# Scan stage of a hybrid block: the normalised inputs join the output product on TensorE instead of being summed into X by GpSimd, and four inputs are turned at other units

## What is computed

```python
def _L0_attn_b_ref(x, W_in, conv_w, conv_b, W_x, W_dt, b_dt, A_log, D, W_out):
    residual = x
    h = x
    for i in range(N_LAYERS):
        h = _mamba_layer(h, W_in[i], ...)
    return h + residual
...
x = x + _L0_attn_b_ref(_layernorm(x, axis=-1), ...)
```

```python
xz = jnp.einsum('bld,ed->ble', x, W_in)
u, z = jnp.split(xz, 2, axis=-1)
u = _silu(_causal_conv1d(u, conv_w, conv_b))
x_dbl = jnp.einsum('bld,rd->blr', u, W_x)
dt, Bm, Cm = jnp.split(x_dbl, [DT_RANK, DT_RANK + D_STATE], axis=-1)
dt = jax.nn.softplus(jnp.einsum('blr,dr->bld', dt, W_dt) + b_dt)
# per state n of 16: h = exp(dt*A)*h + dt*B*u ;  y = sum over n of h*C
y = _selective_scan(u, dt, A, Bm, Cm, Dvec)
y = y * _silu(z)
return jnp.einsum('bld,od->blo', y, W_out)
```

## Time and profile before

| | us |
|---|---|
| median of 3 runs | 2099.44 (2098.75 to 2099.64) |
| the profiled execution, its own time | 2099.91 |
| span of the profiled execution | 2098.1 |
| attention and first mixture of experts | 0 to about 764 |
| scan stage | about 764 to 1551 |
| second mixture of experts | 1551 to the end |

### The profile page before, as it was taken

How to read it: one execution, slowest core, us unless ns; L and a number is a source line. 1 busy time by engine, 2 the same in 40 slices (tenths; PEclk the granted TensorE clock), 3 DMA queues, 4 the chain that set the end, 5 groups by cost and what they waited for, 6 DMA issues and landing times. The chain is left out here.

```text
span 2098.1 us, 43518 instructions
## 1 busy us (share of the span) xinstructions
PE 2017.1 (96%) x14806; PEld 1576.1 (75%) x14807; DVE 1455.4 (69%) x2683; ACT 1202.9 (57%) x2403; POOL 1439.2 (69%) x973
## 2 busy tenths in 40 slices
PE   7999999999999989999999999999799999999998
PEld 5887447999999736666676666666564499999994
DVE  6887685333333389999999999999976733333335
ACT  5775522222222259999999999999853232222222
POOL 6775004777777439999999999999940077777760
PEclk9999999999999999999999999999999999999999
DMA  8000100000000344433444334333343000000014
GB/s 312 1 0 2 41 1 15 25 25 25 25 25 24 83 123 119 112 103 113 113 112 114 122 112 112 107 112 108 102 178 116 3 25 25 25 25 25 24 24 124
DMA packets 94714, 151.21 MB, mean 72 GB/s; under 512 B 27611, under 2 KB 61789, under 8 KB 92422
## 3 DMA queue, kind: packets, MB, share of 16 engines
q1 hardware_dynamic: 85510, 131.10, 20.7%
q0 software_dynamic: 9088, 18.63, 3.1%
...
## 5 line engine op out<-in xcount | busy, mean ns | idle before, releaser
L2413 POOL TENSOR_TENSOR m_seen<-m_state,experts 128x1024 f32<-128x1024 f32 (+1 forms) x256 | 598.8, 2375 | 12.3 <-DVE m_state L2468 10.3
L2468 DVE TENSOR_TENSOR_SCAN m_state<-experts,ps 128x512 f32<-128x512 f32 x448 | 537.2, 1233 | 1.9 <-issue 1.3
L1940 PE MATMUL ps<-ident,m_seen 128*128 128x128 f32 x2040 | 270.5, 276 | 23.7 <-POOL m_seen L2413 23.6
L2204 ACT ACTIVATE experts<-delta,experts 128x512 f32<-128x512 f32 x448 | 291.4, 713 | 0.3
L1940 PEld LDWEIGHTS ps<-ident,m_seen 128*128 128x128 f32 x2040 | 234.6, 142 | 63.1 <-POOL m_seen L2413 45.0
L1600 POOL COPY f_weights<-experts 128x1898 f32 x142 | 252.5, 1778 | 23.8 <-issue 23.5
L1421 PE MATMUL first_up_ps<-f_xT,f_weights 128*128 128x128 f32 x1988 | 241.4, 275 | 1.7 <-issue 1.7
L1421 PE MATMUL ps<-zu,f_weights 128*128 128x128 f32 x1988 | 241.4, 275 | 1.7 <-issue 1.7
L1421 PEld LDWEIGHTS first_up_ps<-f_xT,f_weights 128*128 128x128 f32 x1988 | 233.2, 192 | 2.5 <-issue 2.5
L1421 PEld LDWEIGHTS ps<-zu,f_weights 128*128 128x128 f32 x1988 | 233.2, 192 | 2.5 <-issue 2.5
L1588 POOL DMA_INDIRECT f_xin<-tokens,f_take x71 | 70.8, 997 | 153.0 <-DVE f_take L1124 134.6
...
## 6 DMA issues: line engine op xcount, KB each, us to landing
...
```

Source lines behind the costliest of these rows:

```text
L1940: mm = pe.matmul(Y[:, i // 2, at:at + P], seen[:, n % SEEN, h, i * P:(i + 1) * P], ident[:], is_transpose=True, start=(n == 0 and at == 0) ...
L2204: act.activation(PB[n % B_RING][:, h, :] if n in AWAY else dA[:, n % DECAYS, h, :], delta[:, U % 2, h, :], ACT.Exp, scale=decay[:, lhn:lhn ...
L2413: pool.tensor_tensor(seen[:, n % SEEN, :, part], state[:, n % RING, :, part], row.unsqueeze(1).to_broadcast([P, HALF, row.shape[-1]]), ALU ...
L2468: dve.tensor_tensor_scan(state[:, n % RING, h, :], decay_, drive_, before_, ALU.mult, ALU.add).then_inc(s_state, 1)
```

## The change

- `add_input` is gone, on POOL, with its two calls at the head and its six at step 13 of units 0 to 5, and so are the semaphore `s_added` and all waits on it.
- In `project_out` of an upper unit PE adds the normalised input from xT, where it still lies turned: for each of the four tiles a matmul with the turned input as weights and the identity as the moving operand, ahead of the one that adds X. `last_out` gets one such matmul for each of its four tiles.
- Since xT holds one sequence per stream only, the inputs k = 4 to 7 must not overwrite it before the output product of the upper unit that needs the old contents. The table `TURNED_IN` gives the unit in which input k is normalised, turned and copied: k = 2 to 7 in units 0, 1, 4, 6, 8, 10 in place of 0, 1, 2, 3, 4, 5. `columns` waits for that output product.

```diff
@@ -1688,7 +1688,7 @@
                 s_w, s_skipped, s_zero, s_halves, s_first_dt = ts("w"), ts("skipped"), ts("zeroed"), ts("halves"), ts("first_dt")
                 s_stats, s_var, s_std, s_rstd = ts("stats"), ts("var"), ts("std"), ts("rstd")
                 s_exp_A, s_neg_A = ts("exp_A"), ts("neg_A")
-                s_ln, s_added = ts("ln"), ts("added")
+                s_ln = ts("ln")
                 s_side0, s_side1, s_read0, s_read1 = ts("side0"), ts("side1"), ts("read0"), ts("read1")
                 s_silu, s_rows, s_bc, s_rounded, s_less, s_parts = (ts(x) for x in ("silu", "rows", "bc", "rounded", "less", "parts"))
                 s_soft, s_dt, s_dtu = ts("soft"), ts("dt"), ts("dtu")
@@ -1711,6 +1711,7 @@
                 N_UNITS = len(UNITS)
                 STEPS = N_UNITS * NS
                 TURNS = len(lower)
+                TURNED_IN = {k - 2 if k < LEAD + 1 else 2 * (k - 2): k for k in range(2, TURNS)}
 
                 def tokens(s, t):
 
@@ -1756,8 +1757,8 @@
                     if V < N_UNITS:
                         uses0 += [("dt0", V), ("dt1", V), ("gate", V), ("b", V), ("du", V)]
                         uses1.append(("gate", V))
-                    if U + 2 < TURNS:
-                        uses1.append(("turn", U + 2))
+                    if U in TURNED_IN:
+                        uses1.append(("turn", TURNED_IN[U]))
                     if V < N_UNITS:
                         uses1.append(("du", V))
                 uses0.append(("out", N_UNITS - 1))
@@ -1962,6 +1963,11 @@
                                     mm = pe.transpose(SIDES[:, h, i * P:(i + 1) * P], turned[:, at:at + P], ident[:])
                             mm.then_inc(s_back, 1)
 
+                        def input_columns(s, t, i):
+
+                            at = PAD + t % C * SEG + i * P
+                            return xT[:, s, at:at + P]
+
                         def project_out(W):
                             l, s, t = UNITS[W]
                             pe.wait_ge(s_y, W + 1)
@@ -1973,7 +1979,8 @@
                                     for h in range(HALF):
                                         mm = pe.matmul(SIDE0[:, i * P:(i + 1) * P], y[:, h, i * P:(i + 1) * P], out_w[:, l * HALF + h, :], start=(h == 0), stop=(h == HALF - 1))
                                 if W < N_UNITS - 1:
-                                    pe.wait_ge(s_added, min(2 * t + s + 1, TURNS))
+                                    for i in range(TILES):
+                                        pe.matmul(SIDE0[:, i * P:(i + 1) * P], input_columns(s, t, i), ident[:], start=False, stop=False, skip_group_check=True)
                                     mm = pe.matmul(SIDE0, ident[:], X[:, tokens(s, t) * D:tokens(s, t) * D + SEG], start=False, stop=True, skip_group_check=True)
                             mm.then_inc(s_side0, 1)
 
@@ -2042,8 +2049,8 @@
                                     gate(V, 1)
                                 if n == B_TURN:
                                     turn_b(V)
-                            if n == TURN and U + 2 < TURNS:
-                                turn(U + 2)
+                            if n == TURN and U in TURNED_IN:
+                                turn(TURNED_IN[U])
                             if n == DU_TURN and V < N_UNITS:
                                 turn_delta_u(V)
                             if n == SKIP:
@@ -2094,7 +2101,8 @@
                             pe.wait_ge(s_y, LAST_UNIT + 1 + j)
                             for i in range(2):
                                 for h in range(HALF):
-                                    mm = pe.matmul(Y[:, j, i * P:(i + 1) * P], y[:, h, (2 * j + i) * P:(2 * j + i + 1) * P], out_w[:, l * HALF + h, :], start=(h == 0), stop=(h == HALF - 1))
+                                    pe.matmul(Y[:, j, i * P:(i + 1) * P], y[:, h, (2 * j + i) * P:(2 * j + i + 1) * P], out_w[:, l * HALF + h, :], start=(h == 0), stop=False)
+                                mm = pe.matmul(Y[:, j, i * P:(i + 1) * P], input_columns(*UNITS[LAST_UNIT][1:], 2 * j + i), ident[:], start=False, stop=True)
                             mm.then_inc(s_side0, 1)
 
                         def ahead_down(c):
@@ -2123,6 +2131,8 @@
                             at = PAD + t % C * SEG
                             bank, s_side, s_read, nth = (SIDE0, s_side0, s_read0, nth0) if k < 2 else (SIDE1, s_side1, s_read1, nth1)
                             act.wait_ge(s_side, nth["turn", k] + 1)
+                            if t >= C:
+                                act.wait_ge(s_side0, nth0["out", UNITS.index((1, s, t - C))] + 1)
                             act.activation(xT[:, s, at:at + SEG], bank, ACT.Copy).then_inc(s_read, 1)
 
                         def convolved(V, h):
@@ -2245,7 +2255,6 @@
 
                         def normalise(k):
                             l, s, t = lower[k]
-                            act.wait_ge(s_added, k)
                             act.wait_ge(s_shift, 1)
                             for i in range(TILES):
                                 j = tokens(s, t) + i
@@ -2259,7 +2268,6 @@
 
                         def normalise_group():
                             act.wait_ge(s_group_shift, 1)
-                            act.wait_ge(s_added, TURNS)
                             act.wait_ge(s_side1, nth1["turn", TURNS - 1] + 1)
                             for i in range(TILES):
                                 ins = act.activation(xn[:, i * P:(i + 1) * P], X[:, i * D:(i + 1) * D], ACT.Identity, scale=numbers[:, RSTD, i:i + 1], bias=numbers[:, SHIFT, i:i + 1])
@@ -2348,10 +2356,10 @@
                             if V < N_UNITS:
                                 if n in GATED:
                                     gated(V, GATED.index(n))
-                            if n == TURN - 1 and U + 2 < TURNS:
-                                normalise(U + 2)
-                            if n == TURN and U + 2 < TURNS:
-                                columns(U + 2)
+                            if n == TURN - 1 and U in TURNED_IN:
+                                normalise(TURNED_IN[U])
+                            if n == TURN and U in TURNED_IN:
+                                columns(TURNED_IN[U])
                             if n in ACROSS_AT:
                                 m = ACROSS_AT[n] + (NS if ACROSS_AT[n] < n else 0)
                                 if U * NS + m < STEPS:
@@ -2384,12 +2392,6 @@
                         pool.memset(diagonal[0], 0.0)
                         pool.memset(hT[:, :, 0:PAD], 0.0).then_inc(s_hT, 1)
 
-                        def add_input(k):
-                            l, s, t = lower[k]
-                            at = tokens(s, t) * D
-                            wait(pool, s_ln, k)
-                            pool.tensor_tensor(X[:, at:at + SEG], X[:, at:at + SEG], xn[:], ALU.add).then_inc(s_added, 1)
-
                         def drive(G):
                             U, n = divmod(G, NS)
                             pool.wait_ge(s_dtu, U + 1)
@@ -2397,8 +2399,6 @@
                             wait(pool, s_state, (G - DECAYS + 1) * HALF)
                             pool.tensor_tensor(dA[:, n % DECAYS], delta_u[:, U % 2], b_rep[:, AWAY.index(n), :].unsqueeze(1).to_broadcast([P, HALF, SEG]), ALU.mult).then_inc(s_away, 1)
 
-                        add_input(0)
-                        add_input(1)
                         pool.tensor_tensor(conv_w[:, 1], conv_w[:, 1], in_wT[:, DI:2 * DI].unsqueeze(1).to_broadcast([P, TAPS, DI]), ALU.mult).then_inc(s_hT, 1)
                         drive(AWAY[0])
                         for G in range(STEPS):
@@ -2422,8 +2422,6 @@
                             if n == DELTA_U and V < N_UNITS:
                                 pool.wait_ge(s_dt, V + 1)
                                 pool.tensor_tensor(delta_u[:, V % 2], delta[:, V % 2], u(V), ALU.mult).then_inc(s_dtu, 1)
-                            if n == TURN and U + 2 < TURNS:
-                                add_input(U + 2)
                             if U == N_UNITS - 1 and n == GROUP_STATS:
                                 group_statistics(pool, numbers, s_group, s_group_shift, summed[0] + TILES)
 
@@ -2435,7 +2433,6 @@
 
                         def normalise(k):
                             l, s, t = lower[k]
-                            dve.wait_ge(s_added, k)
                             for i in range(TILES):
                                 ins = layernorm(dve, xn[:, i * P:(i + 1) * P], tokens(s, t) + i)
                             ins.then_inc(s_ln, 1)
@@ -2533,7 +2530,6 @@
                         dve.wait_ge(made.s_down, 1)
                         ahead_product(dve, made, 2)
                         _, s, t = UNITS[LAST_UNIT]
-                        dve.wait_ge(s_added, TURNS)
                         for j in range(2):
                             at = tokens(s, t) + 2 * j
```

## The result

The changed kernel took 2100.77 us in the median of 22 runs (2098.09 to 2105.47), the kernel before 2097.63 us in the 22 runs beside it (2094.57 to 2101.40). The ratio is 1.0016, with a 95% interval from 1.0010 to 1.0022: about 3.4 us slower, and less than the 0.2% that I had set as the bound of "no change". The profiled execution took 2100.88 us, with a span of 2098.8. The forecast of 2100.2 stood against a kernel before of 2099.44; what it says of the change is +0.74 us, and that is 2.5 us too little.

What follows compares the result with a forecast made beforehand. No engine has room in the scan loop, so waits between engines set each unit's period. Terms -4.96 +2.06 +1.58 +1.09 +0.97 = +0.74 on 2099.91, less 0.47 for the median: 2100.2 us; range 2095.4 to 2104.0.

Steps and rivals of the forecast that it cites:

- GpSimd's sums: Scan loop: six sums at step 13 of units 0 to 5 go, 1.24 us each where GpSimd is the bound.
- 0→1: Period from unit 0's step-9 sum into delta to unit 1's: sum worth the 0.86 us gate wait, 47.91 to 47.05.
- 4→5: Period from unit 4's step 9 to unit 5's: sum goes, turn stays, at first -1.24 us.
- 2→3, 3→4, 5→6: Periods between step 9 of those units, which lose sum and turn: -1.24, -1.32 and -1.41 us.
- Moved turns: Turns leave units 2, 3, 5 for 6, 8, 10: +1.30 us in unit 6, -0.19 in unit 8, 0 in 10.
- Added matmuls: Upper units' output products at step 5: eight more passes, 0.97 us, delaying GpSimd's step-9 sum; +2.06 us in six units.
- Both together: Late ScalarE makes the turn later in units 6, 8 (+0.44 us) and 4, 10 (+1.14): +1.58 us.
- Head and tail: Stage's start: DVE's first statistic behind GpSimd's longer product, +1.09 us; last output product, 16 to 24 passes: +0.97.
- the second: Rival: added matmul passes come through whole, 0.97 us in each of six units, +4.50, 2103.9 us; chance 0.15.
- the third: Rival: one more fall of TensorE's clock in a bound unit of the loop, 2101.7 us; chance 0.10.
- The first: Rival: PE's added passes are covered before step 9, head perhaps free too, -3.99, 2095.4 us; chance 0.17.
- The fourth: Rival: moved turns cost nothing because GpSimd is behind anyway at steps 14 and 15, 2092.8 us; chance 0.05.

Runs made afterwards that it cites:

- e1: The kernel before without add_input's sums into X and their waits, turns unmoved, no added matmuls, normalised input left out of the result: 2097.11 us, ratio 0.9994.
- e2: The changed kernel without the added matmuls, normalised input left out of the result: 2097.73 us, ratio 1.0000.
- e3: The changed kernel with GpSimd's product on conv_w at the head waiting until VectorE's variances are done: 2099.92 us, ratio 1.0013.

## Why the prediction was right or wrong

- **The time** of 2100.2 lies 0.6 from the 2100.77 measured, partly by luck: the kernel before came out 1.8 us lower in the longer series than in the three runs I started from, and the change cost 3.1 to 3.4, not 0.74. Its class, within 0.2%, was right.
- **GpSimd's sums**, the step that failed. "The sum is worth what DVE waited at the gate, 0.86" for 0→1: it gained nothing. The wait in front of the gate product was ScalarE's work for the turned input, one link behind TensorE; "it waits so only when GpSimd is behind" was wrong. In 4→5 the sum was costed at 1.24, the distance between 2→3 and 10→11. But unit 2 has a sum and a turn and unit 10 neither, so this is the price of both: 0.82 for the sum (e1) and 0.43 for the turn (e2), which I had put at nothing. The missed amounts are 0.87 in 0→1, 0.62 in 4→5 and 0.60 in 10→11, 2.1 us, nearly all that the loop came out above the forecast apart from the clock.
- **2→3, 3→4, 5→6**: right in size, by comparing units of like kind, and not in the reason. What I took for turn and sum together in 3→4 and 5→6 was the turn alone, and what I took for the sum alone in 2→3 was 0.81 of sum and the rest turn (e1).
- **Moved turns**: 6→7 +1.44 for 1.52 forecast (turn and delay), and 1→2 unchanged; right. A new wait at the gate from unit 6 on, named as a sign of being wrong, is there but small: behind the moved turns TensorE stands 0.49 (units 7 and 9) and 0.63 (unit 11) for ScalarE at step 4, and VectorE 0.16 more at most.
- **Added matmuls**: 5→6 and 7→8 are 0.15 above the forecast, 3→4 and 9→10 within 0.03. In fresh even units the delay of TensorE comes through by 0.89, in continuing ones by 0.1, as the rooms in the earlier trace rows said. The first row that shows it, VectorE's stand at step 8, was not on my list, and step 9's room was not the place.
- **Both together**: too small. The matmuls cost 0.75 in 4→5 and 10→11 (e2), on top of 0.43 for the turn itself; I had 0.57 for the two. The 0.1 in the periods ahead, 3→4 and 9→10, is thus only what shows first.
- **The clock**: I counted the fall in 8→9 as gained (1.49 of the 48.57, so that the turn there came out at -0.19). It is no property of that unit. The changed kernel had two, in units 11 and 13.
- **Head and tail**: +0.91 and +0.88 for 1.09 and 0.97. For the head the cleaner figure is the first scan's +0.88, since the falls of the clock behind it move the head by up to 1.1. The mechanism is shown by e3's 0.21 us. The rule of the Trainium skill that the forecast weighed (SBUF — State Buffer, section on the two separate sides) agrees with the trace: VectorE's instruction ended with GpSimd's in both kernels.
- **The rivals**: in size the second, matmuls that come through whole (+4.50), and the third, one more fall of the clock (+2.2), lie about equally far from the 3.1 to 3.4 measured. The third has one fall more in the profiled run for it; whether the changed kernel has more of them in most runs is not shown. Of the second: the matmuls came through nearly whole in four units of six, in 6 and 8 at once and in 4 and 10 through the turn behind them, and by 0.14 in 12 and 14. The first is out: they are not covered, and e2, which has none of them, is no faster than the kernel before. The fourth is out too, since 6→7 pays 1.44 for its turn.
